# A graph network's second layer on one core: layer norm, transposes and first projections in five node groups

## What is computed

```python
h = relu(layernorm(x))                       # per node, 256 features
ei = concat([h[src], edge_attr])
msg = sigmoid(ei @ Wg + bg) * (relu(ei @ W1 + b1) @ W2 + b2)
out = segment_sum(msg, dst) + h
x = x + layernorm(out) * gamma + beta        # end of layer 0

h = relu(layernorm(x))                       # layer 1 begins
proj_f = einsum('ni,rio->rno', h, Wf)        # 16 relations forward, 16 backward
proj_b = einsum('ni,rio->rno', h, Wb)
m_forward  = segment_sum((proj_f[type, src] + fbias) / indegree[dst], dst)
m_backward = segment_sum((proj_b[type, dst] + bbias) / outdegree[src], src)
x = x + 2 * (h @ loop_weight) + self_bias + m_forward + m_backward
```

## Time and profile before

| | us |
|---|---|
| median of 3 runs | 3950.99 |
| lowest, highest | 3943.87, 3952.12 |
| profiled execution | 3952.31 |
| its span | 3950.5 |
| PE busy in the span | 3321.7 (84%) |
| DVE busy | 2648.6 (67%) |
| POOL busy | 2309.3 (58%) |
| ACT busy | 1032.2 (26%) |

### The profile page before, as it was taken

One profiled execution on the slowest core, in us unless ns is written; L12 is line 12 of the kernel. 1 busy time (PEld: TensorE's weight loads), 2 busy tenths in 40 slices (PEclk: granted clock), 3 DMA queues, 4 the chain that ended last, 5 costly groups with the idle time before them and its releaser, 6 DMA issues.

```text
span 3950.5 us, 70214 instructions
## 1 busy us (share of the span) xinstructions
PE 3321.7 (84%) x18784; PEld 2867.6 (73%) x18785; DVE 2648.6 (67%) x3870; ACT 1032.2 (26%) x1671; POOL 2309.3 (58%) x2362
## 2 busy tenths in 40 slices
PE   6999999999999993899677778778867778787776
PEld 5999999999999993688456556566655666665654
DVE  6999999999999996777566765334354444444444
ACT  3555555555555553344000000000010000000000
POOL 1555555555555550000677676777777777777775
PEclk8999999999999996999888999999989999999999
DMA  5666666666666650465555556555533333333333
GB/s 178 186 186 186 186 184 184 185 182 182 183 182 178 182 168 14 144 211 208 150 155 158 146 154 160 168 157 160 162 109 105 105 100 99 102 103 105 105 105 114
DMA packets 325878, 595.62 MB, mean 151 GB/s; under 512 B 77030, under 2 KB 196436, under 8 KB 325716
## 3 DMA queue, kind: packets, MB, share of 16 engines
q0 software_dynamic: 137984, 411.19, 37.2%
q1 hardware_dynamic: 185868, 180.03, 14.1%
q10 hardware_dynamic: 1864, 2.52, 0.2%
HBM read 478.12 MB, written 115.41 MB: 150 GB/s over the span
## 4 chain that ended last, share of the span: by engine, by line
PE 68%; DVE 12%; issue 10%; POOL 3%; DMA 3%; DVEq 3%; ACT 1%; ACTq 0%; SPq 0%; POOLq 0%
PE pc L648 13%; PE pa L657 13%; PE pa L696 7%; PE pu L696 4%; PE pg L623 4%; PE pu L630 4%; PE pu L759 4%; PE pu L634 4%; PE pg L759 4%; PE pg L696 4%; POOL fa L412 3%; DVE tops L1154 3%; PE pc L643 2%; DVE key L1157 2%; DMA fa<-proj,gslot 2%
## 5 line engine op out<-in xcount | busy, mean ns | idle before, releaser
L412 POOL DMA_INDIRECT fa<-proj,gslot x1568 | 1500.9, 957 | 950.8 <-issue 435.7
L395 POOL DMA_INDIRECT fa<-ptab,slot x784 | 804.6, 1026 | 641.2 <-issue 323.8
L657 PE MATMUL pa<-fa,onehot 128*128 128x258 f32 x1760 | 466.3, 412 | 239.7 <-DVE onehot L964 163.3
L648 PEld LDWEIGHTS pc<-ws,hr 128*128 128x128 f32 x4704 | 608.5, 188 | 17.7
L648 PE MATMUL pc<-ws,hr 128*128 128x256 f32 x4704 | 615.8, 280 | 0.0
L964 DVE SCALAR_TENSOR_TENSOR fa<-pc,base,src_f 128x512 f32<-128x512 f32 x406 | 303.6, 751 | 449.6 <-PE pa L696 327.2
L657 PEld LDWEIGHTS pa<-fa,onehot 128*128 128x128 f32 x1760 | 345.6, 202 | 346.3 <-issue 293.1
L696 PE MATMUL pa<-fa 128*128 128x258 f32 x1568 | 374.4, 381 | 0.0
L696 PEld LDWEIGHTS pa<-fa 128*128 128x128 f32 x1568 | 297.6, 190 | 45.4
L696 PE MATMUL pu<-fa 128*128 128x258 f32 x784 | 200.0, 398 | 119.9 <-DVE acc L1021 74.1
L485 ACT CAST hr<-fa 128x1024 fp32r<-128x1024 f32 x196 | 206.3, 1053 | 308.3 <-DVE fa L970 296.6
(11 more groups left out here) (147 smaller groups left out, 5058.7 us busy)
## 6 DMA issues: line engine op xcount, KB each, us to landing
proj<-fa SPq DMA_DIRECT2D x400, 256.0 KB, 2.4
fa<-in_ea_t SPq DMA_DIRECT2D x392, 128.0 KB
fa<-proj,gslot POOLq DMA_INDIRECT x1568, 2.8
fa<-ptab,slot POOLq DMA_INDIRECT x784, 3.7
fa<-in_Wrel SPq DMA_DIRECT2D x32, 256.0 KB, 3.0
ptab<-fa SPq DMA_DIRECT2D x25, 256.0 KB, 2.0
out<-res SPq DMA_DIRECT2D x4, 768.0 KB
res<-in_x SPq DMA_DIRECT2D x1, 1792.0 KB, 20.5
```

Source lines behind the costliest of these rows:

```text
L395: pool.indirect_dma_start(pbuf[:, n % 2, j, :], None, ptab[:, :], bass.IndirectOffsetOnAxis(ap=slot[:, n, j:j + 1], axis=0)).then_inc(s_ga ...
L412: pool.indirect_dma_start(gbuf[:, n, j, 0:H], None, proj[k - 1][:, :], bass.IndirectOffsetOnAxis(ap=gslot[:, at, j:j + 1], axis=0)).then_i ...
L648: last = nc.tensor.matmul(pc[:, j, :], uT[:, par, a, kk, j * P:(j + 1) * P], w2s[:, c, kk, :], start=False, stop=(j == jj + 1 and n == 2 a ...
L657: last = nc.tensor.matmul(pa[:, bank, 0:width], keys[:, at, j, :], rows[:, j, :], start=(n == 0), stop=(n == len(todo) - 1))
```

## The change

- The 25 blocks of layer norm 1, residual, layer norm 2, transposes and the projections of relation 0 are done in five groups of GB = 5 blocks. DVE's loop takes in group g: statistics 1, scales 2 of group g - 1, centring and residual of g, low halves of the transposed blocks of g - 1, statistics 2 of g. ACT's `node_group` interleaves normalising and high halves of group g - 1 with the evacuation of the projections of g - 2. PE transposes a group and then projects it.
- Layer norm 1 is no longer normalised on ACT: DVE subtracts the mean, multiplies by gamma (`centre`), then multiplies by 1/std and adds to `res` (`residual`), one instruction a block each.
- beta is added to `res` in layer 0 already: 13 blocks before the first supertile, 12 before the last `messages`.
- The transposes of layer 1 have three banks (`turned`) instead of two; the iota copy, which shares one, goes behind them.
- The self product goes behind all forward projections on PE, its add behind `take_rows` on DVE, in `pa` instead of `pu`. The self bias is added before it.
- The sort of relations 0 and 1 goes behind the pipeline, with the low weights of relation 2 ahead of both.

The diff, cut (the lines of the diff's `wait_ge` arguments for the groups and the added semaphore are left out):

```diff
+        def turned(k, b):
+            bank = (pa[:, 0, 0:H], pa[:, 1, 0:H], pc[:, 2, :])[b % (3 if k else 2)]
+            return bank.rearrange("p (k n) -> p k n", k=HK)
...
 @block.scalar
-            sqrt_var(1)
-            for b in range(NB):
-                normalise(1, b, acc, ACT.Identity)
-            sqrt_var(2)
...
-            for b in range(NB):
-                normalise(2, b, res, ACT.Relu)
-                if b >= 1:
-                    transposed_high(b - 1)
-            transposed_high(NB - 1)
...
-            weights_high(0, 0, 0)
-            relations(0, True, every=True)
+            def node_group(g):
+                if g < NB // GB:
+                    sqrt_var(1, g, GB * g, GB * (g + 1))
+                if g == 0:
+                    weights_high(0, 0, 0)
+                for n in range(GB + 1):
+                    if 1 <= g <= NB // GB and n < GB:
+                        normalise(2, group(g - 1)[n], res, ACT.Relu)
+                    if g >= 2 and n >= 1:
+                        evacuate(act, nc.scalar.copy, 0, group(g - 2)[n - 1])
+                    if 1 <= g <= NB // GB and n >= 1:
+                        transposed_high(group(g - 1)[n - 1])
+                if g < NB // GB:
+                    sqrt_var(2, g, GB * g, GB * (g + 1))
+                elif g == NB // GB:
+                    weights_high(1, 1, 0)
+
+            for g in range(NB // GB + 2):
+                node_group(g)
+            weights_high(2, 0, 1)
+            for b in range(NB):
+                evacuate(act, nc.scalar.copy, 1, b)
...
 @block.tensor
                 pe.wait_ge(s_h[2 * k], b + 1)
-                if b >= 2:
-                    pe.wait_ge(s_hT[k], b - 1)
+                buffers = 3 if k else 2
+                if b >= buffers:
+                    pe.wait_ge(s_hT[k], b - buffers + 1)
...
-            transposes(1, 0)
-            for b in range(NB):
-                if b + 1 < NB:
-                    transposes(1, b + 1)
-                own(b)
-            pe.wait_ge(s_selfadd, NB)
...
-            forward_relations(0)
+            for g in range(NB // GB):
+                for b in group(g):
+                    transposes(1, b)
+                if g == 0:
+                    pe.wait_ge(s_wlo, 1)
+                for b in group(g):
+                    pe.wait_ge(s_hT[1], b + 1)
+                    project(0, 0, b, 0)
+            pe.wait_ge(s_wlo, 2)
+            for b in range(NB):
+                project(1, 1, b, 0)
             with pe.Fori(1, NQ // 4) as i:
                 forward_relations(i)
 
+            pe.wait_ge(s_split, 2)
+            for b in range(NB):
+                own(b)
+            pe.wait_ge(s_selfadd, NB)
             for n, w in enumerate(windows_of(pe, 0, 0, GS)):
                 sum_projections(1, n, n, 0, w)
...
 @block.vector
+            def add_beta(b0, b1_):
+                part = res[:, b0:b1_, :]
+                link(nc.vector.tensor_tensor(part, part, beta_b[:, :].unsqueeze(1).to_broadcast([P, b1_ - b0, H]), ALU.add))
+
+            add_beta(0, NB // 2 + 1)
             features_low(0, 0)
...
             add_further(ST - 3, 1, w[0])
+            add_beta(NB // 2 + 1, NB)
             messages(ST - 1, 1)
...
-            link(nc.vector.tensor_copy(iota_p, iota[:, :]))
-            ln_statistics(1, acc)
-            ln_scales(1)
-            a, g = acc[:, :, 0:H], lambda t: t[:, :].unsqueeze(1).to_broadcast([P, NB, H])
-            dve.wait_ge(s_h[1], NB)
-            link(nc.vector.tensor_tensor(a, a, g(gamma_b), ALU.mult))
-            link(nc.vector.tensor_tensor(a, a, g(beta_b), ALU.add))
-            nc.vector.tensor_tensor(res[:, :, :], res[:, :, :], a, ALU.add).then_inc(s_x1, 1)
-            dve.wait_ge(s_x1, 1)
-            ln_statistics(2, res)
-            ln_scales(2)
...
-            for b in range(NB):
-                evacuate_hT(1, b)
-                if b >= 1:
-                    add_own(b - 1)
-            add_own(NB - 1)
...
+            def centre(g):
+                dve.wait_ge(s_var[1], g + 1)
+                for b in group(g):
+                    last = nc.vector.scalar_tensor_tensor(out=acc[:, b, 0:H], in0=acc[:, b, 0:H], scalar=mv[:, b, 0:1],
+                                                          in1=gamma_b[:, :], op0=ALU.subtract, op1=ALU.mult)
+                link(last)
+
+            def residual(g):
+                dve.wait_ge(s_std[1], g + 1)
+                link(nc.vector.reciprocal(rstd[:, GB * g:GB * (g + 1)], rstd[:, GB * g:GB * (g + 1)]))
+                for b in group(g):
+                    last = nc.vector.scalar_tensor_tensor(out=res[:, b, :], in0=acc[:, b, 0:H], scalar=rstd[:, b:b + 1],
+                                                          in1=res[:, b, :], op0=ALU.mult, op1=ALU.add)
+                last.then_inc(s_x1, 1)
+
+            for g in range(NB // GB + 1):
+                if g < NB // GB:
+                    ln_statistics(1, acc, GB * g, GB * (g + 1))
+                if g == 1:
+                    weights_low(0, 0)
+                if g >= 1:
+                    ln_scales(2, g - 1, GB * (g - 1), GB * g)
+                if g < NB // GB:
+                    centre(g)
+                    residual(g)
+                else:
+                    dve.wait_ge(s_w2, 16)
+                    split([w2s[:, c, :, :].rearrange("p k f -> p (k f)") for c in range(2)], wlraw)
+                    nc.vector.memset(gbuf[:, :, :, H:AW], 1.0).then_inc(s_split, 1)
+                if g >= 1:
+                    for b in group(g - 1):
+                        evacuate_hT(1, b)
+                if g < NB // GB:
+                    dve.wait_ge(s_x1, g + 1)
+                    ln_statistics(2, res, GB * g, GB * (g + 1))
+            weights_low(1, 1)
+            dve.wait_ge(s_hT[1], NB)
+            link(nc.vector.tensor_copy(iota_p, iota[:, :]))
+            link(nc.vector.memset(ones_c[:, :], 1.0))
+            nc.vector.memset(acc[:, :, :], 0.0).then_inc(s_zero[0], 1)
+            nc.vector.tensor_tensor(res[:, :, :], res[:, :, :], sbias_b[:, :].unsqueeze(1).to_broadcast([P, NB, H]),
+                                    ALU.add).then_inc(s_sb, 1)
...
-            weights_low(0, 0)
-            forward_relations(0)
+            weights_low(2, 0)
+            for q in range(2):
+                sort_relation(q)
             with dve.Fori(1, NQ // 4) as i:
                 forward_relations(i)
             sort_rest()
...
             for n in range(0, 2 * GS, 2):
                 take_rows(1, n, n)
+            for b in range(NB):
+                add_own(b)
+            dve.wait_ge(s_selfadd, NB)
             w = windows_of(dve, 0, 0, GS)
```

More of the change, by code:

```diff
@@ L28 @@
 XA = 10
+GB = 5
 TS = 4
@@ L830, in add_own @@
                 dve.wait_ge(s_self, b + 1)
-                last = nc.vector.scalar_tensor_tensor(out=res[:, b, :], in0=pu[:, b % 2, 0:H], scalar=2.0,
+                last = nc.vector.scalar_tensor_tensor(out=res[:, b, :], in0=pa[:, b % 2, 0:H], scalar=2.0,
                                                       in1=res[:, b, :], op0=ALU.mult, op1=ALU.add)
@@ L1163, in keep_sorted, with sort_relation @@
                 nc.vector.tensor_copy(srt[:, bass.ds(8 * it, 8 * n)], tops[:, 0:8 * n]).then_inc(s_sort, 1)
+            def sort_relation(q):
+                before = (2 * S1 + 1) * q
+                for n in range(S1):
+                    sort_step(before + 2 * n, n)
+                keep_sorted(before + 2 * S1, S1 * q, S1)
             def forward_relations(i):
@@ L1167, in forward_relations @@
                     weights_low(2 * i + u + 1, 1 - u)
-                    before = (2 * S1 + 1) * (2 * i + u)
-                    for n in range(S1):
-                        sort_step(before + 2 * n, n)
-                    keep_sorted(before + 2 * S1, S1 * (2 * i + u), S1)
+                    sort_relation(2 * i + u)
             def sort_rest():
```

49 lines of the change are left out of this document (22 added, 27 removed).

## The result

The changed kernel took 3892.03 us (median of 4 runs, 3887.88 to 3897.86), the kernel before 3951.27 on the same chip: a ratio of 0.9855, 95% interval 0.9838 to 0.9873, thus 59.2 us (1.5%) faster; by the interval the gain is 50 to 64 us. Run again on another chip, it gained 55.1 us (3946.55 to 3891.41). The forecast was 3898. The profiled execution of after took 3890.98 us (span 3889.2).

The account below looks back on a forecast made before the run. PE bound the forward projections, after two holes on PE (layer norms, self bias); DVE started the gather stage. 3952.3 - 55.8 (earlier slot copies) + 3 (self product) = 3899.5, median 1.3 below: 3898; range 3882 to 3920.

Parts of the forecast that it names:

- S: Start of the fifth, last projecting phase of the layer-norm pipeline on PE; predicted at 1571.9 us on the profile's clock.
- DVE's price of a group: Layer-norm pipeline: DVE's statistics, scales, centring, residual and low halves for five blocks, 11.1 us a group.
- The loop: Pipeline round on PE: 4.6 us transposing plus 9.0 us projecting, each projecting phase starting at half clock: 13.6 us.
- rival B: Pipeline: every projection runs at half clock, phases 13.65 us, loop 18.3; gain 34.1 us, time 3920; chance 0.12.
- Rival A: Pipeline: the clock stays full, phases 6.8 us, loops 11.4 from the second on; gain 62.4 us, time 3891.6; chance 0.20.
- The two nearly equal loops: Pipeline: DVE's loop of 11.7 us and PE's of 11.4 at full clock are nearly equal, so the clock decides.
- Gain of the slot copies: End of the forward stage: DVE's slot copies (L1202) start at 1826.9 instead of 1882.7, gain 55.8 us.
- Self product: Behind all projections on PE: delays the first gathered sum, POOL stalls 2.3 us at its seventeenth gather; taken as 3 us.
- Rival C: Self product at its new place gives back 10 to 15 us in place of 3; time 3908; chance 0.12.
- Edits costed at nothing: ten square roots' table loads taken as 0 (bound about 10 us); beta adds in layer 0 covered (6.8 us uncovered).
- D: Pipeline: queues tie groups together, engines work one behind the other, 30 us a group; time 3963; chance 0.04.
- E: Pipeline: the edit is none, transposes still wait for the whole norm; nothing is won, time 3951; chance 0.04.

## Why the prediction was right

- **What bounds what.** The two holes on PE closed but for the first 13.1 us, and PE's forward stage and the gather stage stayed as they were. The chain from PE to DVE's sort to the slot copies was read rightly: they come at S + 254.2, predicted S + 255. PE waited nowhere in the forward stage but once, 0.47 us. At relation 3 less was in hand than predicted: the low weights were ready at 1640.38 and PE came to them at 1640.77, so 0.4 us instead of 1.5, because relation 0 ended at S + 6.9, not S + 9. A small slip beside it: the terms up to the start of the sort add up to S + 18.7, not S + 18; measured S + 18.6.
- **DVE's price of a group.** Predicted 11.1 us; the busy times of the DVE lines sum to 11.0: centring and residual 10.3 us for 25 each, so 0.41 a block, predicted 0.40 (481 ns is the duration of one, and they overlap), aggregates 4.5 in place of 3.5 in all, low halves and statistics as in the earlier trace rows.
- **The loop: the mis-sized term.** Predicted 13.6 us, measured 12.3 (12.05 to 12.5 in every profile with five blocks a group). A projecting phase was to take 9.0 us each time: it takes 8.5 where it begins at half clock (1.5 us lost, where I had 2.2) and 7.0 where it does not, and of the four later phases only two or three begin so (in after two). The transposing phase was to take 4.6 us: it takes 4.0, or 4.6 to 4.9 behind some of the phases at full clock. In after the projecting phases of the four rounds average 8.0 us, which is 1.0 of the 1.3 us, and the transposing phases 4.25, which is the rest. So the four rounds took 49.1 us, not 54.9; with a first phase 1.2 us earlier (0.75 of it because the stretch began earlier than the 1498.6 of the prediction) S was 1564.9, predicted 1571.9. The rule of the Trainium skill ("TensorE: Matmul & The Clock Gate", Loop structure matters more than you think), that matmuls behind a long wait in every round of a loop run cold, holds here for some of the phases and in these for the first twelve matmuls (4.59 us against 3.00), not for whole phases. So rival B's condition was not met.
- **Rival A's numbers came by luck.** Rival A gives S = 1565.3 and 3891.6 us, and 1564.9 and 3892.0 were measured. Its mechanism did not happen: the clock did not stay full, and its loop of 11.4 us was 12.3. Its second phase starts at 1531.1, taken from the forecast, where 1527.85 was measured, and three rounds that are too short make up for it.
- **The two nearly equal loops.** PE's loop of 4.6 + 9.0 was the right sum, and "so the clock decides" is half of the truth. A phase at full clock is 1.5 us shorter, but in after PE then waits 1.93 us for DVE, and the round is only 0.6 us shorter (11.92 against 12.54). Neither closer casts nor idle work for the clock shortened the round; the waits moved between DVE, ScalarE and PE. DVE's 11.0 us of work are its floor, and the 1.1 to 1.5 us above it were not taken away by any run here. What would take them away stays open.
- **Gain of the slot copies.** Predicted 55.8 us, measured 63.7: 7.0 by S, 0.8 by the rest of the way. (The prediction counts from 1498.6, and the stretch of after began 0.75 us earlier; so much of it is the spread of layer 0.)
- **Self product.** T is the start of the slot copies. Predicted: first sum done at T + 25.3 and a stall of 2.3, taken as 3. Measured: first sum added at T + 26.1, seventeenth gather at T + 27.3, stall 4.3; without the self product it is 0. In the sum, PE's rest of the self product was right (T + 20.5, predicted 21.5), while I had one_hot follow it at once: the last add, one_hot and their handing over keep PE idle for 2.28 us in front of the first sum, and that sum, at low clock, is added 3.4 us after its first matmul, where I had 2.0. Rival C (10 to 15) did not come.
- **Edits costed at nothing.** Table loads: two at the root's line, as before, right. Beta: first part covered, second part costs 0.9 of 3.35 us, because PE's work on the last supertile came at full clock in after (granted clock 1.00 from 1486 to 1492; before 0.79, 0.50 and 0.85) and the cover was 2.7 instead of 4.1 us.
- **The total.** -63.7 + 4.3 = -59.4, measured -59.2 on the medians and -55.1 on the second chip. Against the forecast of -52.8 the earlier S and the rest of the way brought 7.8 us and the self product took 1.3.
- **Rivals D and E.** D's one behind the other did not happen (round 12.3, not 30). E's condition is what one group makes, and its price was wrong: that kernel takes 3914.7, not 3951, since the self product's new place and the smaller layer norm count without any overlap.
- **What I had not seen.** Beyond the prediction, DVE's 12.2 us of memset and self bias now stand on the path's last leg, and 7.0 us of idle time on PE ahead of the self product with them. The prediction had "PE sets it or DVE, within 1.2 us" for this place, and took that for a balance, not for a chance: moved to POOL, with the sort put ahead of the weights, they were worth 9 us more on one chip (on the fourth the stage shows it, the time doesn't).

## What to carry to other kernels

When a stage of whole-tensor steps is cut into groups over several engines, price each engine's round together with the waits inside it (here PE's 7.0 to 8.5 us of projections and 4.0 of transposes at the others' pace). In this one case the real round was 10 to 14% above the dearest engine's work, and the waits between nearly balanced engines changed hands when one was made shorter. Choose the group by its shared and handing-over costs: one block a group cost 16.9 us for five here, five blocks 12.3, and 25 blocks gave the overlap away. After the change look again at what sets the next stage: an engine that was hidden (here DVE's sort with a memset and an add ahead of it) becomes the path, and relief there pays only together with the order of the work behind it (by the stage's clock 1 to 2 us for each alone, 9 together).

## What the runs showed of the hardware

- With groups of one block PE waits about 1.0 us in front of each block's projections and 0.3 us in front of its transposes, is busy 12.59 of 20 us, and its granted clock is 1.00. With groups of five, after transposing phases of 4.0 to 4.9 us, two or three of the four later projecting phases begin at half clock.
- In after no idle time of PE in the transposing phase ahead of the second projecting phase is longer than 0.81 us, and still the clock falls to half 0.6 us into the projections, with PE busy (granted clock 0.97 from 1528.0 to 1528.5, 0.50 behind that; the phase starts at 1527.85).
- The pattern in which the phases of a loop begin at half clock differs from one profile of the same kernel to another (second and fourth; first, third and fifth), with S equal within 0.8 us.
- POOL needs 14.3 us for the add of 128x6400 that takes DVE 6.76, and 5.49 for the memset of 128x6450 that takes DVE 5.43. Neither changed the duration of DVE's sort steps (978 ns).
- On the other chip sixteen gathers are issued in the same 20.7 us, but POOL then waits 16 to 21 us, where the first chips show 0.3 to 4.7; the stretch from layer norm to slot copies takes the same time on both (321.2 and 321.3 us, changed kernel and the one without beta).
